# First attention of a fused attention and transformer kernel: score matmuls of 63 and 64 rows instead of 48 and 49

## The chip, the cores and the metric

One core of one Trainium2 chip runs the whole program in one launch. The metric is device time in microseconds (us); lower is better. Engines: PE is TensorE (matmul; PEld are its weight loads), DVE is VectorE, ACT is ScalarE, POOL is GpSimd, SP is SyncE, which only issues DMAs here.

## The reference, cut to what matters

Eight sequences of 512 tokens and 256 channels go through an attention layer with 16 heads of 16 channels, then (not touched here) through two layers of local attention and gated feed-forward.

```python
qkv = x @ w_qkv + b_qkv
q, k, v = jnp.split(qkv, 3, axis=-1)          # 16 heads of 16
a = jnp.einsum('bhsd,bhtd->bhst', q, k)
a = (a + causal_mask) / np.sqrt(HEAD_DIM)
a = jax.nn.softmax(a, axis=-1)
z = jnp.einsum('bhst,bhtd->bhsd', a, v)
z = z.transpose(0, 2, 1, 3).reshape(B, S, D)
...
x = _layernorm(x + z @ w_out + b_out)
```

## The kernel before, in words

**Split operands.** Products that must be close to float32 are made of operands in two parts, high and low. For the scores of the first attention the three products (high by high, high by low, low by high) are stacked along the contraction rows: `Q` holds 16 rows of q high, 16 of q high, 16 of q low, and `Kk` holds k high, k low, k high. These are the slots; `SLOTS = 48` rows hold them. Two heads stand beside each other on the partitions, the even one from row 0, the odd one from row `ODD = 64`. Both tiles have 8 pairs of heads in their second dimension.

**Two passes over the scores.** Step `sm` (L573 to L595 of PE) multiplies one block of 128 queries of a pair by all keys it may see, 48 rows deep (L588, two matmuls, one per head), adds the causal mask by four bfloat16 matmuls of 64 rows (L594), and DVE takes the negative maximum of each row (L468). When the eight blocks of four heads are done, step `mt` turns the maxima on PE (L620), ACT copies them to `mrow` (L421), and SP writes them by four DMAs (L290) into one further row of `Q`, row 48 (and 112), where `Kk` has a row of ones, set by POOL at the start (L322; it sets rows 32 to 63 and 96 to 127 to 1.0, and the slots' loads overwrite 32 to 47). So step `st` (L633, L638), 49 rows deep, gives the transposed scores already shifted by the maximum; ACT takes their exponential into `PT` (L430), POOL zeroes what lies above the diagonal (step `ms`, L345), and step `pv` multiplies by V, 32 matmuls for four heads (L660).

**What sets the order.** The work of all engines is one list of steps written out by hand, `STEPS`; a step `f_...` belongs to the next sequence. Every engine walks the same list with its own part of each step, and semaphores join them. The loop over sequences runs seven times over the list; a first piece (`FIRST`) stands ahead of it and a last one behind. `f_qk` and `f_v` project (L527 to L529), `f_qe` writes q and k parts to `scr` (L265, L267), `f_load` reads them back into `Q` and `Kk` as slots (L283), `z0` to `z3` normalise and turn, `out` projects (L675, L677). `wait_ge(v_set, 3)` holds SP's first load back until DVE's initial memsets are done (V twice, and the padding columns of `Q`, L446).

```python
ODD, SLOTS = 64, 48
...
rows = slice(ODD * hh, ODD * hh + SLOTS)          # sm
...
rows = slice(ODD * hh, ODD * hh + SLOTS + 1)      # st
```

Of the kernel before, what the change touches and what calls it, by code (L numbers as in the profile page):

```python
# [7 lines left out]
F32 = mybir.dt.float32  # L8
# [12 lines left out]
NB, S, DM = 8, 512, 256  # L21
# [36 lines left out]
def wait_apart(eng, K, sem, value):  # L58


    if not isinstance(value, int):
        value = eng.snap(eng.to_reg(value))
        eng.wait_ge(K["made"], MADE)
    eng.wait_ge(sem, value)
# [65 lines left out]
def first_attention(nc, K, scr, w, xin, rows_out, zeros, ahead, x, w_qkv, b_qkv, w_out, b_out, dst):  # L130

    with ExitStack() as ctx:
# [4 lines left out]
        def sem(name):  # L137
            signals.append(nc.alloc_semaphore(name="a_" + name))
            return signals[-1]
# [10 lines left out]

        ODD, SLOTS = 64, 48
        Q, Kk = sb("Q", [P, AH // 2, S + P], F32R), sb("K", [P, AH // 2, S], F32R)

        tri = sb("tri", [P, 2, P], BF16)
# [45 lines left out]
        v_set = sem("v_set")  # L202
# [27 lines left out]
        def steps(eng, do, tail=None):  # L230
            for name, i in FIRST:
                do(name, i, 0)
            with eng.Fori(0, NB - 1) as it:
                for name, i in STEPS:
                    do(name, i, it + 1 if name[0] == "f" else it)
            for name, i in STEPS:
                if name[0] != "f":
                    do(name, i, NB - 1)
                    if tail is not None:
                        tail(name, i)  # L240

        with nc.Block() as block:
            @block.sync
            def _(sp):
                sp.dma_start(xin[:, :, :], x[0].rearrange("(t p) d -> p t d", p=P)).then_inc(x_in, 16)
                for k in range(KT):
                    sp.dma_start(w_raw[:, k, :], w_qkv[P * k:P * k + P]).then_inc(w_loaded[k], 16)
                for n in range(2):
                    sp.dma_start(bqk[:, n::2], b_qkv[DM * n:DM * n + DM].rearrange("(h p) -> p h", p=P),
                                 allow_slow_non_contiguous=True).then_inc(b_loaded, 16)  # L250
                sp.dma_start(bv[:, :], b_qkv[2 * DM:].partition_broadcast(P)).then_inc(b_loaded, 16)
                sp.dma_start(bo[:, :], b_out.partition_broadcast(P)).then_inc(b_loaded, 16)
                wo_rows = w_out.rearrange("(g j d) n -> j d g n", j=HP, d=AD)
                for r in range(2 * HP):
                    sp.dma_start(wo[AD * r:AD * r + AD, :, :], wo_rows[r // 2]).then_inc(wo_loaded, 16)

                def do(name, i, b):
                    if name == "f_x":
                        if not isinstance(b, int):
                            sp.wait_ge(front_full, (b - 1) * NF + 2)  # L260
                            sp.dma_start(xin[:, :, :], x[b].rearrange("(t p) d -> p t d", p=P)).then_inc(x_in, 16)
                    elif name == "f_qe":

                        sp.wait_ge(front_free, b * NE + 1 + i)
                        sp.dma_start(scr[b, 0, P * i:P * i + P], qk_hi[:, i, :].bitcast(F32)).then_inc(parts_out, 16)  # L265
                        sp.wait_ge(lo_done, b * 4 + 1 + i)
                        sp.dma_start(scr[b, 1, P * i:P * i + P], qk_lo[:, i, :].bitcast(F32)).then_inc(parts_out, 16)  # L267
                    elif name == "f_load":

                        wait_apart(sp, K, parts_out, b * 128 + 64 * (i // 2 + 1))  # L270
                        if i == 0 and isinstance(b, int):
                            sp.wait_ge(stacks_set, 2)
                            sp.wait_ge(v_set, 3)
                        if not isinstance(b, int):

                            sp.wait_ge(sc_full, 2 * ((b - 1) * EU + GE * (i + 1)))
                        r0, t0 = 64 * (i % 2), 2 * (i // 2)
                        for t, dst_t, order in ((t0, Q, (0, 0, 1)), (t0 + 1, Kk, (0, 1, 0))):
                            for slot, part in enumerate(order):
                                rows = scr[b, part, P * t + r0:P * t + r0 + 64].rearrange("(h e d) n -> e d h n", e=2, d=AD)  # L280
                                for hh in range(2):
                                    at = ODD * hh + AD * slot
                                    sp.dma_start(dst_t[at:at + AD, PG * i:PG * i + PG, 0:S].bitcast(F32), rows[hh])\  # L283
                                        .then_inc(stacked[i], 16)
                    elif name in ("mt", "f_mt"):
                        sp.wait_ge(mrow_done, b * AG + i + 1)
                        for hh in range(2):
                            at = ODD * hh + SLOTS
                            for p in range(PG):
                                sp.dma_start(Q[at:at + 1, PG * i + p, 0:S].bitcast(F32),  # L290
                                             mrow[2 * p + hh:2 * p + hh + 1, i, :].bitcast(F32)).then_inc(m_in[i], 16)

                def tail(name, i):
                    if (name, i) == FIRST_OF_LAST:
                        sp.wait_ge(parts_out, NB * 128)
                        sp.wait_ge(lo_done, NB * 4)
                        ahead.load(sp, ahead_raw, ahead_wo)
                        zeros.store(sp)
                        sp.wait_ge(front_full, NB * NF)
                        sp.wait_ge(stored, 16)  # L300
                        ahead.first(sp)
                    elif name == "end":
                        zeros.done(sp)

                steps(sp, do, tail)

            @block.gpsimd
# [134 lines left out]
            def _(dve):  # L442
# [6 lines left out]
                def do(name, i, b):  # L449
                    if name == "f_xe":  # L450
# [4 lines left out]
                        if isinstance(b, int):  # L455
                            for kt in range(KT):
                                dve.wait_ge(w_split, kt + 1)
                                dve.tensor_tensor(w_lo[:, kt, :], w_raw[:, kt, :], w_hi[:, kt, :], ALU.subtract)\
                                    .then_inc(w_low, 1)
                    elif name in ("sm", "f_sm"):  # L460
                        p, q = i // TB, i % TB
                        nk = P * (q + 1)
# [48 lines left out]
                def tail(name, i):  # L511
                    if (name, i) in LOW:
                        ahead.low(dve, ahead_raw, ahead_wo, LOW.index((name, i)))
                    elif name == "end":
                        dve.wait_ge(rstd_done, NB)
                        dve.wait_ge(stored, 16 * NB - 16)
                        for t in range(TB):
                            dve.tensor_scalar(out[:, t, :], y[:, t, :], mv[:, t, 0:1], rs[:, t:t + 1],
                                              ALU.subtract, ALU.mult).then_inc(out_done, 1)

                steps(dve, do, tail)

            @block.tensor
            def _(pe):
# [6 lines left out]
                def bank_wait(done, b, units, i, hh):  # L531

                    if not (isinstance(b, int) and b == 0 and i == 0):
                        pe.wait_ge(done, 2 * (b * units + i) + hh - 1)

                def do(name, i, b):
# [37 lines left out]
                    elif name in ("sm", "f_sm"):  # L574
# [9 lines left out]
                            pe.wait_ge(tri_set, 4)  # L584
                            pe.wait_ge(K["made"], MADE)
                        for hh in range(2):
                            rows = slice(ODD * hh, ODD * hh + SLOTS)
                            pe.matmul(bank[:, hh, 0:nk], Q[rows, p, P * q:P * q + P], Kk[rows, p, 0:nk],  # L588
                                      start=True, stop=True)

                        for n in range(2):
                            for hh in range(2):
                                rows, at = slice(ODD * hh, ODD * hh + ODD), P * q + ODD * (hh ^ n)
# [29 lines left out]
                    elif name in ("st", "f_st"):  # L623
# [3 lines left out]
                        if i % GE == 0:  # L627
                            pe.wait_ge(m_in[i // GE], b * 64 + 64)
                        for hh in range(2):
                            rows = slice(ODD * hh, ODD * hh + SLOTS + 1)  # L630
                            bank_wait(exp_done, b, EU, i, hh)
                            if t < 2:
                                m = pe.matmul(SC[hh][:, 0:S - P * t], Kk[rows, p, P * t:P * t + P], Q[rows, p, P * t:S],  # L633
                                              start=True, stop=True)
                            else:
                                for j in (2, 3):
                                    at = 2 * P * (j - 2)
                                    m = pe.matmul(SC[hh][:, at:at + 2 * P], Kk[rows, p, P * j:P * j + P],  # L638
                                                  Q[rows, p, P * j:P * j + 2 * P], start=(j == 2), stop=True,
                                                  skip_group_check=True)  # L640
                            m.then_inc(sc_full, 1)
# [22 lines left out]
                    elif name == "out":  # L664
# [14 lines left out]
                        m.then_inc(y_full, 1)  # L679

                steps(pe, do)


# [1046 lines left out]
```

## Time and profile before

| | |
|---|---|
| runs | 1996.41, 2001.62, 2005.23 us; median 2001.62 |
| the profiled execution | 1997.55 us, span of its trace 1996.0 us |
| mean granted TensorE clock | 0.922 of full speed |
| busy | PE 90%, DVE 56%, ACT 48%, POOL 47% of the span |
| stages | first attention up to about 515 us, then local attention and feed-forward, twice |

The profiled execution is 4.1 us below the median of the runs. In the page, each digit of a line is the busy share of a fortieth of the span (49.9 us); PEclk is the granted clock in tenths. A granted clock of 1.00 is 2.4 GHz and one of 0.50 is 1.2 GHz; a mean between the two is a stretch that had both.

### The profile page before, as it was taken

To read this page: it belongs to the slowest core of one execution; us is meant where nothing else is said; L and a number is where in the kernel's file an instruction comes from. 1 tells how busy PE (TensorE), PEld (TensorE's weight loads), DVE (VectorE), ACT (ScalarE), POOL (GpSimd) and SP (SyncE) were. 2 spreads that over 40 slices of the span, in tenths; PEclk is the share of its full clock that TensorE was granted. 3 is DMA by queue.
4 is the path that set the end of the run, shared out by engine and by line. 5 is a ranking of instruction groups with operands and counts; after the bars stand their busy time and mean duration, and the time that the engine had idled before them with its cause. 6 is when DMAs were issued, how large, how long until landed. Compare 5 with 4: busy or idle time off the path is not lost. (4 is left out here: it accounts for less than half of the span.)

```text
span 1996.0 us, 42845 instructions
## 1 busy us (share of the span) xinstructions
PE 1787.4 (90%) x14072; PEld 1353.2 (68%) x14072; DVE 1109.8 (56%) x2825; ACT 967.3 (48%) x1898; POOL 934.7 (47%) x923
## 2 busy tenths in 40 slices
PE   5899988898669999999979999599999999789887
PEld 3556655565347777777768888477777777577776
DVE  4566655666467766676523333676676666234343
ACT  2655545554336555555534444265555555333332
POOL 3355444554336655555423333455555555333433
PEclk7898888987779999999979999699999999799998
DMA  4333343334010000000121112100000001121221
GB/s 144 106 115 107 106 122 112 117 109 127 22 33 12 32 32 32 32 32 21 50 58 43 63 63 95 44 12 32 32 32 32 32 21 49 50 70 63 65 74 42
DMA packets 103736, 121.28 MB, mean 61 GB/s; under 512 B 23387, under 2 KB 75781, under 8 KB 103685
## 3 DMA queue, kind: packets, MB, share of 16 engines
q1 hardware_dynamic: 96772, 95.45, 15.7%
q0 software_dynamic: 6912, 25.17, 3.5%
q8 instruction: 29, 0.48, 0.1%
q14 instruction: 23, 0.18, 0.0%
HBM read 82.55 MB, written 37.77 MB: 60 GB/s over the span
## 5 line engine op out<-in xcount | busy, mean ns | idle before, releaser
L468 DVE TENSOR_REDUCE a_negm<-a_x 128x2 f32<-128x256 f32 (+3 forms) x256 | 202.4, 814 | 143.7 <-PE a_x L594 141.5
L430 ACT ACTIVATE a_PT<-a_c 128x384 f32<-128x384 f32 (+1 forms) x384 | 183.7, 522 | 139.7 <-PE a_c L633 84.4
L866 POOL TENSOR_TENSOR work<-work 128x512 f32<-128x512 f32 x128 | 164.5, 1287 | 152.2 <-DVE work L1016 151.0
L1541 DVE SCALAR_TENSOR_TENSOR m_hid<-m_a,mw_b,m_gate 128x512 f32<-128x512 f32 x96 | 71.9, 749 | 244.4 <-ACT m_gate L1479 219.8
L1034 DVE CUSTOM_DVE_ANT_0 l_x<-l_x,window 128x256 f32<-128x256 f32 (+1 forms) x512 | 184.1, 421 | 31.7 <-PE l_x L1131 31.7
L1065 PE MATMUL l_f<-w_hi,tails 128*128 128x512 f32 x384 | 168.8, 440 | 14.2 <-DVE work L1016 11.1
L949 ACT ACTIVATE l_PT<-l_c 128x512 f32<-128x512 f32 (+1 forms) x256 | 125.3, 542 | 87.8 <-PE l_c L1171 84.1
L1436 POOL TENSOR_TENSOR m_hid_lo<-m_hid,m_hid_hi 128x512 fp32r<-128x512 f32 x80 | 102.7, 1291 | 131.3 <-ACT m_hid_hi L1490 131.1
L1066 PE MATMUL l_f<-w_hi,tails 128*128 128x512 f32 x384 | 154.8, 403 | 0.0
L1067 PE MATMUL l_f<-w_lo,tails 128*128 128x512 f32 x384 | 154.1, 401 | 0.0
L880 POOL TENSOR_TENSOR l_PS<-l_PT 128x768 f32<-128x768 f32 x64 | 119.6, 1869 | 58.7 <-ACT l_PT L949 58.7
L1479 ACT ACTIVATE m_gate<-m_g,mw_b 128x512 f32<-128x512 f32 x80 | 54.6, 682 | 185.2 <-PE m_g L1588 185.2
L588 PE MATMUL a_x<-a_K,a_Q 48*128 48x256 f32 (+2 forms) x512 | 119.4, 434 | 18.2 <-DMA a_K<-qk_parts 15.4
L873 POOL TENSOR_TENSOR work<-work,l_inv 128x512 f32<-128x512 f32 x128 | 130.9, 1043 | 0.0
L884 POOL TENSOR_TENSOR l_zl<-l_zt,l_zh 128x512 fp32r<-128x512 f32 x64 | 82.8, 1302 | 100.0 <-ACT l_zh L955 100.0
L345 POOL TENSOR_SCALAR_AFFINE_SELECT a_PT<-a_PT 128x512 f32<-128x512 f32 x128 | 81.0, 657 | 97.1 <-ACT a_PT L430 97.0
L660 PE MATMUL a_f<-a_PT,a_V 128*32 128x512 f32 (+3 forms) x1024 | 101.2, 550 | 26.1 <-POOL a_PT L345 14.8
L916 ACT ACTIVATE work<-l_f 128x512 f32<-128x512 f32 x128 | 76.5, 598 | 91.6 <-PE l_f L1067 72.0
L1188 PE MATMUL l_o<-l_PT,l_V 128*64 128x256 f32 (+1 forms) x1024 | 111.8, 361 | 5.7 <-ACT l_PT L949 5.7
L1011 DVE TENSOR_REDUCE l_ss<-work 128x8 f32<-128x512 f32 x128 | 87.0, 680 | 38.8 <-ACT work L916 38.3
L1065 PEld LDWEIGHTS l_f<-w_hi,tails 128*128 128x128 f32 x384 | 74.3, 194 | 44.4 <-issue 21.8
L633 PE MATMUL a_c<-a_Q,a_K 49*128 49x512 f32 (+1 forms) x256 | 94.3, 518 | 7.3 <-DMA a_Q<-a_mrow 3.1
(240 smaller groups left out, 5091.8 us busy)
## 6 DMA issues: line engine op xcount, KB each, us to landing
a_Q<-qk_parts SPq DMA_DIRECT2D x192, 64.0 KB, 2.1
a_K<-qk_parts SPq DMA_DIRECT2D x192, 64.0 KB, 2.1
qk_parts<-a_qk_hi SPq DMA_DIRECT2D x32, 256.0 KB, 2.1
qk_parts<-a_qk_lo SPq DMA_DIRECT2D x32, 256.0 KB, 2.2
after_attn<-rows_out POOLq DMA_DIRECT2D x16, 512.0 KB, 5.2
xin<-after_attn SPq DMA_DIRECT2D x32, 256.0 KB, 3.1
m_xr<-after_attn SPq DMA_DIRECT2D x16, 512.0 KB, 4.1
xin<-in_L_attn_x SPq DMA_DIRECT2D x8, 512.0 KB, 3.5
```

Source lines behind the costliest of these rows:

```text
L430: nc.scalar.activation(PT[:, p // PG % 2, 2 * (p % PG) + hh, QOFF[t]:QOFF[t] + nq], SC[hh][:, 0:nq], ACT.Exp, scale=AD ** -0.5).then_inc(e ...
L468: dve.tensor_reduce(negm[:, q, 2 * p:2 * p + 2], MX[i % 2][:, :, 0:nk], AX.X, ALU.max, negate=True).then_inc(max_done, 1)
L588: pe.matmul(bank[:, hh, 0:nk], Q[rows, p, P * q:P * q + P], Kk[rows, p, 0:nk], start=True, stop=True)
L866: pool.tensor_tensor(t1[:, par, w, :], t1[:, par, w, :], t2[:, par, w, :], ALU.add)\
L873: pool.tensor_tensor(qk[:, i, w, :].rearrange("p (h d) -> p h d", d=FD), t1[:, par, w, :].rearrange("p (h d) -> p h d", d=FD), inv[:, par, ...
L880: pool.tensor_tensor(PS[:, i % 2], PT[:, i % 2, :, 1:TB, 0:P], PT[:, i % 2, :, 0:TB - 1, P:2 * P], ALU.add).then_inc(ps_done, 1)
L949: nc.scalar.activation(PT[:, p % 2, hh, j:j + 2, :].rearrange("p j q -> p (j q)")[:, 0:nq], SC[hh][:, 0:nq], ACT.Exp, scale=8.0).then_inc( ...
L1034: m = dve.tensor_tensor_reduce(out=o, in0=o, in1=mask, scale=-1.0, scalar=-NEG, op0=ALU.add, op1=ALU.min, accum_out=negm[:, q + t, p // 2, ...
L1065: pe.matmul(o, a_hi, r_hi, start=first, stop=False)
L1066: pe.matmul(o, a_lo, r_hi, start=False, stop=False)
L1067: return pe.matmul(o, a_hi, r_lo, start=False, stop=last)
L1188: pe.matmul(OB[rows, P * j:P * j + nq], V[:, j, FD * h:FD * h + FD], PT[:, i % 2, hh, j, 0:nq], start=(j == 0), stop=(j == TB - 1), skip_g ...
```

## The change

`SLOTS` goes; the shift moves to row 63 (and 127), `SHIFT = 63`. Step `sm` reads rows 0 to 62 (64 to 126), step `st` rows 0 to 63 (64 to 127). DVE writes zeros into rows 32 to 63 and 96 to 127 of `Q` once, before the first load, so rows 48 to 62 of `Q` are zero from then on; `Kk` holds ones there already. The values computed are the same. SP's first load waits for the two new memsets. The list of steps is as before.

```diff
-        ODD, SLOTS = 64, 48
+        ODD, SHIFT = 64, 63
...
                             sp.wait_ge(stacks_set, 2)
-                            sp.wait_ge(v_set, 3)
+                            sp.wait_ge(v_set, 5)
...
-                            at = ODD * hh + SLOTS
+                            at = ODD * hh + SHIFT
...
                                     .then_inc(w_low, 1)
+                            for at in (32, ODD + 32):
+                                dve.memset(Q[at:at + 32, :, 0:S].bitcast(F32), 0.0).then_inc(v_set, 1)
...
-                            rows = slice(ODD * hh, ODD * hh + SLOTS)
+                            rows = slice(ODD * hh, ODD * hh + SHIFT)
...
-                            rows = slice(ODD * hh, ODD * hh + SLOTS + 1)
+                            rows = slice(ODD * hh, ODD * hh + ODD)
```

The one place where an engine's sequence changes is the start of DVE. Its rows of the changed program (the numbers after L are lines of the changed file, 2 or so further down):

```order
L446 MEMSET a_Q 128x8x128
L118 MEMSET zero_row 8x64
L453 TENSOR_TENSOR a_xt_lo<-a_f,a_xt_hi 128x512 x2
L458 TENSOR_TENSOR w_lo<-a_PT,w_hi 128x768 x2
L461 MEMSET a_Q 32x8x512 x2
L470 TENSOR_REDUCE a_negm<-a_x 128x2 x4
```

The row with `32x8x512 x2` is new; before, the first reduction followed `w_lo` directly. All other engines issue what they issued, in the same order.

## Rows read from the trace of the kernel before

**Rows 1.** The page, busy time and the 40 slices: PE and the granted clock.

```profile
PE 1787.4 (90%) x14072; PEld 1353.2 (68%) x14072; DVE 1109.8 (56%) x2825; ACT 967.3 (48%) x1898; POOL 934.7 (47%) x923
...
PE   5899988898669999999979999599999999789887
...
PEclk7898888987779999999979999699999999799998
```

**Rows 2.** Two passes: us; PE, PEld, DVE, ACT, POOL busy; PEclk, DMA share, GB/s.

```profile
176.98:237.90 60.92, 54.76 (x493) 35.52 (x489) 38.09 (x65) 33.63 (x71) 30.66 (x36) 0.89 0.37 112
237.90:299.94 62.04, 55.76 (x492) 35.62 (x488) 38.42 (x65) 33.61 (x71) 30.63 (x36) 0.86 0.37 110
```

**Rows 3.** The same view of the longer stretches at the lower clock.

```profile
93.10:99.90 6.80, 6.80 (x44) 3.83 (x47) 4.97 (x7) 4.57 (x9) 2.27 (x4) 0.50 0.35 90
...
212.60:222.80 10.20, 10.20 (x74) 6.02 (x78) 5.41 (x8) 5.54 (x11) 2.44 (x4) 0.50 0.32 86
...
489.20:499.30 10.10, 8.19 (x52) 3.35 (x50) 2.60 (x3) 2.89 (x6) 6.19 (x9) 0.50 0.16 53
```

**Rows 4.** The same view: stretches before and after changes of the clock.

```profile
209.30:212.50 3.20, 2.19 (x18) 1.39 (x18) 2.41 (x4) 2.12 (x5) 2.78 (x5) 1.00 0.44 164
212.60:215.90 3.30, 3.30 (x25) 2.70 (x25) 2.01 (x4) 2.07 (x4) 0.00 (x0) 0.50 0.45 124
216.10:219.40 3.30, 3.30 (x31) 2.15 (x33) 2.05 (x4) 2.38 (x6) 1.22 (x2) 0.50 0.38 103
...
260.50:263.80 3.30, 2.28 (x30) 1.54 (x30) 1.78 (x4) 0.97 (x3) 0.00 (x0) 1.00 0.71 228
263.90:270.60 6.70, 5.04 (x36) 1.88 (x36) 2.22 (x3) 1.60 (x3) 1.27 (x1) 0.50 0.34 83
1793.10:1796.30 3.20, 2.72 (x11) 2.54 (x12) 0.75 (x1) 1.44 (x3) 1.68 (x2) 0.50 0.39 118
1796.50:1799.80 3.30, 3.30 (x16) 2.54 (x15) 0.18 (x1) 0.99 (x2) 1.74 (x1) 1.00 0.08 24
```

**Rows 5.** PE's groups from 212.6 to 215.9 us, shapes apart.

```profile
L588 PE MATMUL a_x<-a_K,a_Q 48*128 48x256 f32 x3 | 1.5, 520 | 0.0
L633 PE MATMUL a_c<-a_Q,a_K 49*128 49x384 f32 x2 | 1.2, 686 | 0.0
```

**Rows 6.** PE's groups from 1793.1 to 1796.3 us, shapes apart.

```profile
L1610 PE MATMUL m_f<-ident,m_hn 128*128 128x128 f32 x8 | 2.0, 427 | 3.2 <-ACT m_hn L1464 3.2
L1586 PE MATMUL m_a<-m_ht_hi,w_hi 128*128 128x512 f32 x1 | 0.8, 776 | 0.0
```

**Rows 7.** PE's groups from 226.3 to 236 us, at the full clock.

```profile
L588 PE MATMUL a_x<-a_K,a_Q 48*128 48x256 f32 x4 | 0.6, 321 | 0.0
```

**Rows 8.** PE's groups from 650 to 800 us, at the full clock (local attention).

```profile
L1131 PE MATMUL l_x<-l_KH,l_QH 64*128 64x256 f32 x84 | 10.5, 327 | 0.0
```

**Rows 9.** Timeline of the pass from 177 us: turning, V products, a mask.

```profile
216.69 1.01 PE L620 MATMUL a_f<-ident,a_negm 128*4 128x128 f32 x4
...
219.32 4.08 PE L660 MATMUL a_f<-a_PT,a_V 128*32 128x512 f32 x32
...
219.97 1.22 POOL L345 TENSOR_SCALAR_AFFINE_SELECT a_PT<-a_PT 128x512 f32<-128x512 f32 x2 [1.68 <-ACT a_PT L430]
...
223.84 2.36 PE L660 MATMUL a_f<-a_PT,a_V 128*32 128x512 f32 x32
...
226.13 0.60 PE L620 MATMUL a_f<-ident,a_negm 128*4 128x128 f32 x4
```

**Rows 10.** DVE at the start of the program.

```profile
8.01 1.83 DVE L458 TENSOR_TENSOR w_lo<-a_PT,w_hi 128x768 fp32r<-128x768 f32 x2
27.86 2.30 DVE L468 TENSOR_REDUCE a_negm<-a_x 128x2 f32<-128x256 f32 x3 [18.03 <-PE a_x L594]
```

**Rows 11.** SP's queue at the start of the program.

```profile
19.86 2.67 SPq L283 DMA_DIRECT2D a_Q<-qk_parts  x6
```

**Rows 12.** POOL's memsets of K, grouped.

```profile
L322 POOL MEMSET a_K<- 32x4096 f32 x2 | 7.0, 3506 | 0.1
```

## The prediction, made before the changed kernel was run

> **What bounds the kernel now.** I read the page first. PE is busy 90% of the span, every other engine at most 56% [rows 1]. PE's digits are 9 nearly everywhere after slice 12. In slices 2 to 10, the first attention, they are 8 and 9 too, but PEclk there is mostly 8: the clock falls inside a stage in which PE is hardly idle [rows 1]. So the next view is the busy time by stretches. One pass of the loop takes 60.9 or 62.0 us at a mean clock of 0.89 or 0.86; ACT and DVE are busy 34 and 38 us of it [rows 2]. PE is therefore what a pass waits for most of the time, and it is slowed by its clock.
>
> Cutting the stage where the clock changes shows one long stretch at 1.2 GHz per pass, always in the same work: the last score steps of a pass, the turning of the maxima and the V products of step `pv` 2. There are eight: the first is 6.8 us, the six of the loop passes behind it are 10.1 or 10.2 us like the second one shown, the last is 10.1 us [rows 3]. In all but the last PE is busy to the full. It isn't idle and then slow; it is slow while it has work.
>
> **Why it is slow there.** Two neighbouring facts are what the forecast rests on. From 212.6 to 215.9 us PE is busy 3.30 of 3.30 us at 1.2 GHz, and the clock stays down for the next stretch [rows 4]. Its matmuls are those of `sm` and `st`, 48 and 49 rows deep, beside the 64-row mask matmuls [rows 5]. From 1793.1 to 1796.3 us, in the last stage, PE is busy less, 2.72 of 3.20 us with only 11 matmuls, and the clock is at 2.4 GHz right behind it [rows 4]; these matmuls are 128 rows deep [rows 6]. Being busy thus doesn't explain the clock; how much of the array works does. I read the trace so: what the granted clock follows grows with the rows in use, the shallow score matmuls count for little, and now their stretches neither hold the clock nor bring it back. Before the fall at 212.6 stands the same picture: PE busy 2.19 of 3.20 us with the same shallow matmuls [rows 4]. The change makes 48 rows 63 and 49 rows 64, in just this work, by a third.
>
> The Trainium skill, "TensorE: Matmul & The Clock Gate", says in "What's actually happening" that the clock is set by how busy the PE has been recently, and in "Why this matters for your kernels" that one should avoid gaps between bursts of matmuls. By that rule, read as busy time, the change does nothing, and the sum would be 0; the trace speaks against it, since the clock stays down through 10.20 us in which PE was busy 10.20. It stands below as a rival.
>
> **The change, part by part.** (a) *Deeper matmuls.* The number and the columns of matmuls stay. Does one of 63 or 64 rows take longer than one of 48? At the full clock the 48-row one of 256 columns takes 321 ns [rows 7], the 64-row one of 256 columns in local attention 327 ns [rows 8]: taken as nothing.
>
> (b) *The clock of the eight stretches.* Worked out on the one from 212.6 us. The V products of step `pv` 2 take 4.08 us at 1.2 GHz; those of `pv` 3 just behind, the same 32 matmuls at 2.4 GHz, take 2.36 [rows 9]: 1.7 us gained. The next V products wait for the mask of 219.97 us (1.22 us long), which moves up with the scores [rows 9], so the 1.7 us isn't lost there. Ahead of them lie 6.7 us of scores and turning (212.6 to 219.3). Turning alone would shrink from 1.01 to 0.60 us [rows 9]. But scores are evacuated by DVE and exponentiated by ACT, which are busy 2.01 + 2.05 and 2.07 + 2.38 us there [rows 4]; so the 6.7 us can't go below about 4.5, the busy time of ACT: a gain of 0 (if ACT's and DVE's chain is the bound already) to 2.2. I take the middle, 1.0 rounded down. That is 2.7 us for each of seven stretches; in the last of the eight PE is only busy 8.19 of 10.1 us [rows 3], so I count the V products' 1.7 alone. Sum 7 x 2.7 + 1.7 = 20.6 us. I don't expect every stretch to stay up: `pv` fills only 32 columns for each head and is itself thin, and the stretch may still start after a wait. I keep four fifths: 16.5 us.
>
> (c) *The second fall.* In two of the passes (62.0 us instead of 60.9, [rows 2]) the clock also falls before step `pv` 1: PE waits for loads and is busy 2.28 of 3.30 us, then runs the V products at 1.2 GHz, 5.04 us busy of 6.7 [rows 4]. The matmuls ahead of that fall are again shallow. Kept up, these two passes give the difference, 62.0 - 60.9 = 1.1 us each: 2.2 us.
>
> (d) *The zeros.* Two memsets of 32 x 4096 on DVE. POOL's of that shape take 3506 ns [rows 12]; DVE has none of it before, so I bound it: 3.5 us each if the engines are alike, half of it if DVE writes faster, twice if the two share a path to memory. They begin when `w_lo` is done at 9.84 us [rows 10] and end at 16.9 us (13.3 to 23.9). What waits for them is SP's first load, issued at 19.86 us [rows 11], and behind it the whole first sequence; DVE's own next work comes at 27.86 us, after an idle time of 18 us [rows 10]. Cover: 3.0 us. Cost 0, at worst 23.9 - 19.9 = 4.0 us.
>
> (e) *The shift row* lands on partition 63 instead of 48, by the same four DMAs of the same size in the same place of SP's queue: nothing.
>
> Sum: 16.5 + 2.2 - 0 = 18.7 us. The profiled execution took 1997.55 us, so it would take 1978.9. The median of the runs is 4.1 us above the profiled one; on that scale the forecast is **1983 us**, 0.9% faster. About 0.5%, 10 us, is what a measurement of this kernel can tell from no change.
>
> **Rivals.**
>
> *Nothing changes* (chance 0.21): the clock follows busy time alone, or the rows are counted in coarse groups in which 48 is already 64. Then (b) and (c) are zero: 2001.6 us. For it: row groups of the array are coarse, and the mask matmuls between are 64 deep already. Against it: rows 4 and 5; two heads' matmuls side by side, each counted as 64 rows, would have the whole array working for 10 us, and the clock still stayed down.
>
> *Only part of it counts* (0.13): only the 64-row step `st` weighs more and the 63-row step `sm` does not, or the clock comes back a stretch earlier but falls all the same. Then some half of (b): 2001.6 - 9 = 1993 us.
>
> *Slower: the falls move* (0.05). PE finishes the score steps sooner and then waits longer for what has its own pace: SP's loads, DMA share 0.71 where PE waits before `pv` 1 [rows 4]. The clock then falls in these waits in every pass, and the dense projections behind them, now at 2.4 GHz, start at 1.2. A stretch of 3.3 us fully busy would take 6.6: 3.3 us in each of seven passes, and 1.1 us for `pv` 1 in the five that don't pay it now, 28.6 us against a gain of 16.5: about 2014 us. It decides from the point where a pass loses more than 2.4 us in new slow stretches. Against it: dense projections bring the clock back quickly in the trace, and the waits follow PE's own progress.
>
> **How the numbers follow.** Forecast 0.61, the rivals 0.21, 0.13 and 0.05. Low end: every stretch stays up with the full 1.7 + 2.2 = 3.9 us, 7 x 3.9 + 1.7 + 2.2 = 31 us, from 2001.6: 1970, and 1 more for the spread of the runs: 1969. High end: nothing changes, with the upper edge left out of a spread of 3.6 us: 2003. The likeliest case has its own range of 1969 to 1991. Faster by over 0.5%: 0.92 of the forecast's 0.61, and a third of the partial case's 0.13: 0.60. Slower by over 0.5%: the slower rival, 0.05. Within 0.5%: the rest, 0.35.
>
> **What would show it.** Right: in the page PEclk of slices 2 to 10 at 9 nearly throughout; the stretch of the last score steps and `pv` 2 at 1.00, its V products near 2.4 us instead of 4.1; passes of some 58 to 59 us; the two memsets of 3.5 us each and the first load still at about 19.9 us; the later stages unchanged. Wrong: eight stretches of 10 us at 0.50 as before (the first rival), short ones in half of the passes (the second), or a lower clock in the projections (the third). If the clock is up and the passes still take 61 us, my reading of PE as the bound is what failed.

## The result, and the profile after

The changed kernel takes 1987.33 us (median of 5 runs, 1986.01 to 1988.42), the kernel before 2001.62 us; the ratio is 0.9936 with a 95% interval of 0.9918 to 0.9953. A second measurement beside the experiments gave 0.9937 (0.9923 to 0.9950), 1987.39 against 1997.57 us. So 10 to 14 us were gained by the one or the other median, 13 us by the ratio. The profiled execution took 1988.02 us, 9.5 less than that of before. One execution of e4 below (2216.92 us, mean granted clock 0.721) and one of e10 (2427.11 us, 0.638) were in a slow state of the chip and are left out of the ratios.

The page after, lines as in [rows 1]:

```profile
PE 1776.7 (89%) x14072; PEld 1345.0 (68%) x14072; DVE 1116.5 (56%) x2827; ACT 968.0 (49%) x1898; POOL 934.4 (47%) x923
...
PE   5889998899679999999979998699999999788887
...
PEclk7898988998789999999979999799999999799998
```

In the first twelve slices PEclk rose by one digit in slices 5, 9, 10 and 12, in and just behind the first attention, and fell in none. The later stages have their old digits but for slice 26, where a stage ends; it reads 7 instead of 6 in e1 below too, which has no deeper matmul. Passes of the loop (us of the stretch and its length; PE, PEld, DVE, ACT, POOL busy; granted clock, DMA share, GB/s), as in [rows 2]:

```profile
57.10:117.60 60.50, 55.62 (x488) 35.26 (x488) 36.59 (x58) 33.23 (x69) 23.52 (x29) 0.87 0.36 106
...
178.00:236.40 58.40, 53.11 (x493) 33.83 (x489) 37.94 (x65) 33.59 (x71) 30.60 (x36) 0.94 0.39 117
...
296.90:357.70 60.80, 54.53 (x490) 35.26 (x488) 38.00 (x65) 33.53 (x71) 30.61 (x36) 0.89 0.37 113
357.70:417.20 59.50, 51.97 (x494) 33.75 (x488) 38.13 (x65) 33.60 (x71) 30.60 (x36) 0.94 0.38 115
```

The first pass in the kernel before, for comparison:

```profile
56.66:116.35 59.69, 54.94 (x489) 34.52 (x489) 36.51 (x58) 33.07 (x69) 25.05 (x30) 0.89 0.36 108
```

The six passes against their lengths before: 60.5 us (59.7 before), 60.4 (60.6), 58.4 (60.9), 60.5 (62.0), 60.8 (60.9), 59.5 (62.0). The first one is thus 0.8 us longer and its clock lower, the second and fifth gained next to nothing, and 6.6 us of gain came in the third, fourth and sixth. The same view of a stretch in the first pass and of the end of the passes, as in [rows 3]:

```profile
80.00:90.30 10.30, 8.46 (x62) 3.77 (x62) 3.83 (x5) 2.83 (x5) 1.27 (x1) 0.50 0.46 142
...
151.70:161.90 10.20, 10.10 (x68) 6.88 (x72) 6.79 (x9) 7.05 (x15) 3.32 (x6) 0.50 0.30 83
213.50:223.70 10.20, 10.15 (x125) 5.87 (x129) 8.56 (x13) 6.36 (x13) 3.79 (x7) 1.00 0.37 95
274.70:281.30 6.60, 6.60 (x50) 3.59 (x52) 4.14 (x6) 3.83 (x8) 2.44 (x4) 0.50 0.27 72
332.70:342.80 10.10, 10.10 (x74) 5.85 (x77) 5.37 (x7) 5.33 (x11) 2.44 (x4) 0.50 0.36 89
394.20:400.80 6.60, 6.60 (x48) 3.97 (x50) 5.22 (x7) 4.70 (x10) 1.78 (x3) 0.50 0.39 108
```

At 213.5 us, in the pass from 178.0, the whole stretch stands at 1.00. At 151.7 and 332.7 us it is as long and as slow as before. At 274.7 and 394.2 us it is 6.6 us instead of 10.1. The stretch at 80.0 us is not of this kind: it is the one in which PE waits for loads and `pv` 1 follows, and in windows of 0.2 us it was 7.0 us long before (79.4 to 86.4). The long stretch of the first pass, at 93.1 us before, is gone.

Where the long stretch is gone in the third and in the last pass, one of 3.4 us at the lower clock has come ahead of it, 28 us into the pass, under the V products of `pv` 1. Here they are in the third pass, before and after:

```profile
204.64 2.36 PE L660 MATMUL a_f<-a_PT,a_V 128*32 128x512 f32 x32 [1.69 <-ACT a_part_f L402]
```

```profile
205.69 3.93 PE L662 MATMUL a_f<-a_PT,a_V 128*32 128x512 f32 x32 [1.70 <-ACT a_part_f L402]
```

PE's groups in the good stretch (compare [rows 5, 7]), and its timeline (compare [rows 9]):

```profile
L635 PE MATMUL a_c<-a_Q,a_K 64*128 64x384 f32 x4 | 1.7, 436 | 0.1
L590 PE MATMUL a_x<-a_K,a_Q 63*128 63x256 f32 x5 | 1.4, 336 | 0.0
```

```profile
217.33 0.60 PE L622 MATMUL a_f<-ident,a_negm 128*4 128x128 f32 x4
...
218.84 2.36 PE L662 MATMUL a_f<-a_PT,a_V 128*32 128x512 f32 x32
...
219.70 1.22 POOL L345 TENSOR_SCALAR_AFFINE_SELECT a_PT<-a_PT 128x512 f32<-128x512 f32 x2 [0.61 <-ACT a_PT L430]
...
221.64 2.36 PE L662 MATMUL a_f<-a_PT,a_V 128*32 128x512 f32 x32
```

The two shapes have their 63 and 64 rows, and 256 columns take 336 ns, where they took 321 with 48 rows in [rows 7]. With more of them the difference goes: in stretches at the full clock `st`'s matmuls of 384 columns take 431 ns with 49 rows (223 to 260 us before) and 430 with 64 (221 to 250 us now), those of 256 columns 328 and 326. Turning takes 0.60 us, where it took 1.01, each set of V products 2.36, and the second begins 2.8 us after the first, where it was 4.5 us. The start of DVE, and of SP's loads (compare [rows 10, 11]):

```profile
7.97 1.83 DVE L458 TENSOR_TENSOR w_lo<-a_PT,w_hi 128x768 fp32r<-128x768 f32 x2
10.71 3.47 DVE L461 MEMSET a_Q<- 32x4096 f32 x1 [0.91 <-issue]
15.09 3.47 DVE L461 MEMSET a_Q<- 32x4096 f32 x1 [0.91 <-issue]
28.14 2.30 DVE L470 TENSOR_REDUCE a_negm<-a_x 128x2 f32<-128x256 f32 x3 [9.57 <-PE a_x L596]
```

```profile
18.04 0.33 SPq L267 DMA_DIRECT2D qk_parts<-a_qk_lo  x1
20.11 2.67 SPq L283 DMA_DIRECT2D a_Q<-qk_parts  x6
```

The memsets take 3.47 us each, with 0.91 us of "issue" ahead of each, and end at 18.56 us. The first load goes out at 20.11 instead of 19.86 us; the store ahead of it (18.04) is itself late by 0.24 us, and the load follows it by 2.07 us, before by 2.06. So it waited for the store and not for the zeros. Where the stage ends is told by the last weight load of `out`, first in the kernel before, then in the changed one:

```profile
L675 PEld LDWEIGHTS a_f<-a_wo_hi,a_zt x128: 186/188/331, 111.0 to 538.9; 128*128 128x128 f32 x128
```

```profile
L677 PEld LDWEIGHTS a_f<-a_wo_hi,a_zt x128: 186/188/330, 111.5 to 529.1; 128*128 128x128 f32 x128
```

538.9 became 529.1 us: the 9.8 us less in the stage are the whole difference of the two profiled executions. Of it 6.0 us came in the six full passes (366.2 us from 56.7 on in the kernel before, 360.1 from 57.1 on now; granted clock 0.87 and 0.90), 4.2 us in the last pass and the piece behind it, and 0.4 us were lost at the start.

### The profile page after: what moved, and what is told of

Read it like the earlier page. It is cut to its first block and busy times, and to the rows that moved or that the text cites. A ratio compares the mean times of both kernels' runs of the same rounds, so it can differ in the third digit from the quotient of the medians.

```text
span 1986.6 us, 42847 instructions
## 1 busy us (share of the span) xinstructions
PE 1776.7 (89%) x14072; PEld 1345.0 (68%) x14072; DVE 1116.5 (56%) x2827; ACT 968.0 (49%) x1898; POOL 934.4 (47%) x923
## 5 line engine op out<-in xcount | busy, mean ns | idle before, releaser
L590 PE MATMUL a_x<-a_K,a_Q 63*128 63x256 f32 (+2 forms) x512 | 114.0, 420 | 16.1 <-DMA a_K<-qk_parts 13.3
L635 PE MATMUL a_c<-a_Q,a_K 64*128 64x512 f32 (+1 forms) x256 | 91.0, 500 | 7.6 <-DMA a_Q<-a_mrow 3.1
```

## The experiments

All ratios are against the kernel before, run on the same chip in turn with it (three chips in all); its median there was 1997.4 to 1998.4 us. The clock is the median over a kernel's executions of the mean granted clock of each; for the kernel before it was 0.923 to 0.924.

| run | what it is | median us | ratio | interval | clock |
|---|---|---|---|---|---|
| e1 | zeros alone, rows 48 and 49 | 1997.43 | 0.9996 | 0.9987 to 1.0005 | 0.924 |
| e2 | `st` 64 rows, `sm` 48 | 1992.78 | 0.9971 | 0.9961 to 0.9981 | 0.928 |
| e3 | `sm` 63 rows, `st` 49 | 1991.40 | 0.9965 | 0.9951 to 0.9979 | 0.928 |
| e4 | 56 and 57 rows | 1991.93 | 0.9968 | 0.9956 to 0.9979 | 0.928 |
| e5 | the changed kernel again | 1987.39 | 0.9937 | 0.9923 to 0.9950 | 0.931 |
| e6 | rows of ones instead of zeros | 1986.20 | 0.9940 | 0.9927 to 0.9954 | 0.933 |
| e7 | masks of 128 rows, on the change | 1995.87 | 0.9988 | 0.9979 to 0.9997 | 0.938 |
| e8 | masks of 128 rows, on before | 2023.85 | 1.0123 | 1.0107 to 1.0138 | 0.918 |
| e9 | `f_sm` 6 to 15 twice, on the change | 1985.97 | 0.9934 | 0.9921 to 0.9947 | 0.938 |
| e10 | the same on before | 1992.35 | 0.9968 | 0.9958 to 0.9978 | 0.930 |
| e11 | `f_sm` 8 to 13 twice, on the change | 1981.78 | 0.9917 | 0.9903 to 0.9930 | 0.938 |
| e12 | `f_sm` 5 to 10 twice, on the change | 1980.49 | 0.9908 | 0.9893 to 0.9924 | 0.939 |

### e1: the zeros without the rows

```diff
-        ODD, SHIFT = 64, 63
+        ODD, SHIFT = 64, 48
...
-                            rows = slice(ODD * hh, ODD * hh + ODD)
+                            rows = slice(ODD * hh, ODD * hh + SHIFT + 1)
```

> Only the two memsets and SP's wait for them; the score matmuls keep 48 and 49 rows, the shift its row 48. Theory (the rows of the score matmuls move the clock): as before, 1996 to 2005 us, with the eight long stretches at the lower clock, 8.0 us at most 10.2 us each. Rival (the change only shifts the work against the clock's own changes, by its 0.3 us later start): near the changed kernel, 1985 to 1990 us, since this start is the same.

1997.43 us, ratio 0.9996. Its page has the granted clock of before, but for one digit less in slice 2 and one more in slices 10 and 26:

```profile
PEclk7798888988779999999979999799999999799998
```

The memsets, SP's wait and the later start cost nothing and gain nothing. The theory's number held, and the rival, that the start 0.3 us later makes the gain, is out.

### e2, e3, e4: one pass alone, and half of the rows

In e2 `sm` reads 48 rows, `ODD * hh` to `ODD * hh + 47`, and everything else is as changed. In e3 the shift is back on row 48, `st` reads 49 rows, `sm` 63:

```diff
-        ODD, SHIFT = 64, 63
+        ODD, SHIFT = 64, 48
...
-                            rows = slice(ODD * hh, ODD * hh + SHIFT)
+                            rows = slice(ODD * hh, ODD * hh + 63)
...
-                            rows = slice(ODD * hh, ODD * hh + ODD)
+                            rows = slice(ODD * hh, ODD * hh + SHIFT + 1)
```

> The transposed scores are 64 rows deep, the first score pass stays at 48. If both passes weigh by their rows, half of the change's 14 us: 1992 to 1996 us. If only the full 64-row pass counts, all of it: 1986 to 1989 us. If only the 63-row pass counts, none: 2000 to 2003 us.

> The first score pass is 63 rows deep, the transposed one stays at 49 with the shift on row 48, so the maximum here is that of scores which contain the previous shift: the shift is not the right one, the instructions and their sizes are. If both weigh by rows: 1992 to 1996 us. If only the 64-row pass counts: 2000 to 2003 us. If only the 63-row pass: 1986 to 1989 us.

0.9971 and 0.9965, so 0.29% and 0.35%, together 0.64%, where the changed kernel has 0.63% (e5). Each figure has an interval of about 0.1% to either side, so that they add up is shown to that width only. Both passes count, the one of 63 rows no less than the one of 64. Their clocks, e2 and then e3:

```profile
PEclk7899888997779999999979999799999999799998
```

```profile
PEclk7888898998789999999979999799999999799998
```

e4 sets `SHIFT = 56` and lets `st` read `SHIFT + 1` rows.

> Rows 56 and 57, the shift on row 56: half of the way from 48 to 63. If the weight grows row by row, part of the gain: 1991 to 1997 us, and a mean clock between 0.922 and 0.933. If rows are counted in groups of 32, the time is that of before (2000 to 2003) or that of the changed kernel (1986 to 1989), nothing between.

0.9968, half of the gain for half of the rows. 48, 49, 56, 57, 63 and 64 all lie between 32 and 64, so a count in groups of 32 would have told no difference between any of these kernels. By the medians, what moves the clock grows with the rows also within such a group; e4's interval (0.9956 to 0.9979) lies clear of e1's and of e5's. Its executions spread widely, from 1989.5 to 1997.5 us, and the profiled one is the slowest of them, with the clock of before (0.922).

### e5, e6: what the rows hold

e6 is the changed kernel with one number:

```diff
-                                dve.memset(Q[at:at + 32, :, 0:S].bitcast(F32), 0.0).then_inc(v_set, 1)
+                                dve.memset(Q[at:at + 32, :, 0:S].bitcast(F32), 1.0).then_inc(v_set, 1)
```

> The changed kernel itself beside the next ones, on the same chip. If the two passes weigh separately and add up (e2 took off 5.7 us and e3 7.0 us against 1998.4), 12.7 us less than before: 1985 to 1988 us.

> As the changed kernel, but rows 48 to 62 of Q hold 1.0 instead of 0.0, against the ones of Kk: each score rises by 15 and so does its maximum, which the softmax takes out again. If the number of rows in use moves the clock: as the changed kernel, 1985 to 1989 us. If what the rows hold counts (zeros being cheap to multiply): off it by more than 3 us, faster if live values raise the clock further, slower if they draw power and cost clock.

0.9937 and 0.9940. Rows of zeros do as much for the clock as rows of ones (0.931 and 0.933). Rows of live values were not tried.

### e7, e8: deeper mask matmuls

```diff
-                        for n in range(2):
-                            for hh in range(2):
-                                rows, at = slice(ODD * hh, ODD * hh + ODD), P * q + ODD * (hh ^ n)
-                                m = pe.matmul(bank[:, hh, at:at + ODD], tri[rows, n, :],
-                                              K["identb"][rows, ODD * hh:ODD * hh + ODD], start=False, stop=True,
-                                              skip_group_check=True)
+                        for hh in range(2):
+                            m = pe.matmul(bank[:, hh, P * q:P * q + P], tri[:, 0, :],
+                                          K["identb"][:, :], start=False, stop=True,
+                                          skip_group_check=True)
```

> As the changed kernel, but the causal mask of step sm comes from two matmuls of 128 rows and 128 columns instead of four of 64 and 64: the same sums. The array takes 128 columns more in each of 256 steps, 53 ns at 2.4 GHz, 13.6 us if PE were the bound in all of them. Theory (rows in use move the clock): the long stretches at 1.2 GHz go in most passes, mean clock of the stage over 0.95, and the time is 1982 to 1992 us, since the clock gives back what the columns take. Rival (busy time alone, or the gain of 14 us was all there is): no better clock, 1994 to 2001 us.

> The kernel before (48 and 49 rows) with the 128-row masks alone. Theory: the clock rises as well though no score matmul is deeper, 1990 to 1998 us. Rival (the effect belongs to the score matmuls' own depth, such as a slower mode of 48-row matmuls): 2000 to 2012 us, with the stretches at the lower clock unchanged.

Both missed in time. e7 lies where its rival put it, but not for its rival's reason: its clock did rise, to 0.938 where the changed kernel has 0.931, and to 0.94 in its loop (57.1 to 420 us). The theory had the clock nearly right there, and not that it would give back what the masks take. e8 lies beyond even its rival: 26 us slower than before by the medians, instead of faster. Passes of e8:

```profile
58.00:123.30 65.30, 62.39 (x427) 34.84 (x426) 38.62 (x62) 34.00 (x71) 25.64 (x30) 0.82 0.33 98
123.30:188.60 65.30, 60.87 (x426) 34.71 (x425) 38.68 (x65) 33.76 (x71) 30.77 (x36) 0.84 0.35 105
188.60:253.60 65.00, 60.86 (x425) 34.61 (x426) 38.63 (x66) 33.76 (x71) 30.75 (x36) 0.84 0.34 105
```

PE is busy 61 of 65 us and the clock is lower than before, 0.82 to 0.84. The timeline of e7 shows one step at 2.4 GHz with its successor, and below it the same steps in the changed kernel:

```profile
226.96 0.28 PE L590 MATMUL a_x<-a_K,a_Q 63*128 63x256 f32 x2
227.17 0.29 PE L594 MATMUL a_x<-identb,a_tri 128*128 128x128 bf16 x2
227.39 0.38 PE L590 MATMUL a_x<-a_K,a_Q 63*128 63x256 f32 x2
```

```profile
224.79 0.28 PE L590 MATMUL a_x<-a_K,a_Q 63*128 63x256 f32 x2
224.92 0.23 PE L596 MATMUL a_x<-identb,a_tri 64*128 64x64 bf16 x4
224.99 0.36 PE L590 MATMUL a_x<-a_K,a_Q 63*128 63x256 f32 x2
```

From the score matmuls of one step to those of the next it takes 0.43 us with 128-row masks and 0.20 us with 64-row ones. The 128 further columns are 53 ns of that at 2.4 GHz. The other 0.18 us come at the two places where PE goes from 64-row matmuls to 128-row ones and back: 0.21 us from scores to mask and 0.22 us from mask to scores, against 0.13 and 0.07. If all 256 steps paid these 0.18 us, it would be 46 us of PE, an estimate from this one step. "TensorEngine Tiling (Array Packing)" of the Trainium skill says in "Key Properties" that changing the tiling mode drains the engine; these rows agree, at some 0.09 us each. So neither run tests cleanly what deeper masks do. In e8 the clock fell though the mask matmuls have twice the rows, which the theory by itself doesn't explain. That the changes of mode are the reason is argued, not shown.

The two runs compared with each other do say something: they differ in the rows of the score matmuls, 48 and 49 or 63 and 64 (and the shift's row and the zeros, which cost nothing in e1). With the deeper ones the kernel takes 1995.87 us instead of 2023.85, 28 us less, at a clock of 0.938 instead of 0.918. That is e5's result again, about twice as large.

### e9 to e12: work of no use, without a change of layout

The next question is whether added work alone moves the clock: issue the step's own score matmuls twice, the second pair over the first (`start=True` begins the sums anew), for some steps of each sequence.

```diff
+                        for again in range(2 if name == "f_sm" and 6 <= i <= 15 else 1):
                             for hh in range(2):
                                 rows = slice(ODD * hh, ODD * hh + SHIFT)
```

e10 is that in the kernel before, at its 48 and 49 rows; e11 has `8 <= i <= 13`, e12 `5 <= i <= 10`.

> As the changed kernel, but the score matmuls of f_sm 6 to 15 are issued twice, the second pair over the first: ten times two matmuls more in each of the eight sequences, work of no use, with 1.5 us of columns in each at 2.4 GHz. Theory (what PE's rows do moves the clock, and the clock is worth 2.5 us a pass where the long stretch goes): the long stretches at 1.2 GHz go in nearly all passes, and the time is 1978 to 1988 us, no slower than the changed kernel in spite of the added work. Rival (the clock isn't what the passes wait for): 1.5 us more for each sequence, 1995 to 2002 us.

> The same doubled matmuls in the kernel before, at 48 and 49 rows. Theory: the clock stays up in more passes as well, 1988 to 1998 us, no slower than before. Rival: 12 us more than before, 2006 to 2014 us.

> As e9, but for f_sm 8 to 13 alone, 0.9 us of columns in each sequence. Theory: between the changed kernel and e9 in its clock, 1980 to 1990 us. Rival: 7 us more than the changed kernel, 1992 to 1996 us.

> As e11, with the doubled score matmuls moved three units up: f_sm 5 to 10, 32 to 37 us after the start of a pass, around the place where the clock fell in the kernel before (35.6 us into its pass) and before most of the stretch. If holding the clock ahead of the fall is what counts, as good as e11 (1981.8 us) or better: 1977 to 1985 us. If the scores inside the stretch must carry it, near the changed kernel: 1985 to 1990 us.

All four medians lie in the theory's ranges. e9 is no faster than the changed kernel (0.9934 and 0.9937): its 160 added matmuls cost nothing. The theory had said that the long stretches would go in nearly all passes, and that missed: in windows of 0.2 us the clock is low for 10.2 us each from 80.6, 200.0, 319.6 and 439.0 us. e11's clock isn't between the changed kernel's and e9's either, but equal to e9's. e10 is the plain case: the kernel before, with nothing but work added, gains 0.32%; its granted clock:

```profile
PEclk7899999898689999999979999799999999799998
```

e11 and e12 add six doubled steps instead of ten, and by the medians gain more than e9; e11's interval overlaps with those of e9 and e5. e12, which puts the steps around the place where the clock used to fall, is the fastest: 1980.49 us, 0.92% below before. Its interval of 0.9893 to 0.9924 only touches e5's 0.9923 to 0.9950, and its five executions (1974.6 to 1981.4 us) all lie below the ten of the changed kernel (1983.1 to 1991.5 us). It ran on another chip than e5, where the kernel before took the same time (1997.36 and 1997.57 us). Its page and three of its passes:

```profile
PE 1767.3 (89%) x14168; PEld 1337.9 (68%) x14168; DVE 1114.9 (56%) x2827; ACT 966.8 (49%) x1898; POOL 934.5 (47%) x923
...
PEclk7899999998689999999979999899999999799998
```

```profile
172.50:230.30 57.80, 51.76 (x501) 33.40 (x502) 37.96 (x66) 33.55 (x71) 30.63 (x36) 0.97 0.39 119
230.30:287.80 57.50, 51.88 (x501) 33.45 (x502) 37.98 (x66) 33.55 (x71) 30.62 (x36) 0.97 0.39 119
287.80:346.50 58.70, 53.67 (x501) 34.30 (x502) 37.93 (x66) 33.61 (x71) 30.61 (x36) 0.94 0.39 117
```

The six passes take 56.9 to 58.7 us at a clock of 0.94 or 0.97, with 12 more matmuls in each. e12 beats both kernels and computes the same. These four runs show that added matmuls can raise the clock and shorten the time. They don't tell rows from busy time, since they add both; that is told by e1 to e4.

## Why the prediction was right, and which term was off

The forecast was 1983 us, 18.7 us gained; 1987.3 was measured, 13 us by the ratio. The direction and the mechanism hold: e1 takes the zeros and the start out of the question, e2 to e4 show the gain growing with the rows while the matmuls' count and columns stay, e6 that rows of zeros and of ones do the same, e10 that the clock can be moved by work alone. The first rival (nothing changes, because busy time or groups of rows are what counts) is out by e2, e3 and e4. The rival "only part of it counts" is out in its first form by e2 and e3, each of which has its half. Its second form, the clock falls all the same, is what happened in some of the passes. The slower rival came in a part of its mechanism, though not in its time: falls moved to `pv` 1, and the first pass is 0.8 us longer. In all, the six full passes gained 6.0 us, where (b) and (c) together had counted 15.2 for them.

- (a) Deeper matmuls cost nothing: right, 430 ns against 431 for 384 columns.
- (b) The value of one stretch, 2.7 us: the pass from 178.0 us is 2.5 us shorter, but not by this sum. The V products of `pv` 2 gave their 1.7 us, 2.36 us for 4.08. The piece ahead of them, from the end of `pv` 1's V products, takes 9.2 us instead of 12.3 (209.6 to 218.8 now, 207.0 to 219.3 before): 3.1 us, where 1.0 was counted. 1.2 us of it are two waits of PE that are gone, 0.80 for the shift's DMA and 0.37 for ACT. Against it `pv` 1's own V products take 1.6 us longer (3.93 for 2.36), and 0.7 us more pass behind the second set. That the sum is near to 2.7 is in part luck.
- (b) "I keep four fifths": this is the step that was mis-sized. Of the eight stretches three are gone (in the first pass, in that from 178.0 and in the one that begins at 417.2), two fell from 10.1 to 6.6 us, and three are still about 10 us long. (The prediction says that all eight lie in the same work. The one at 489.2 us doesn't: it is in the piece behind the loop, under a turning and V products that wait for POOL's mask. And the first one, only 6.8 us long, was counted like those of 10.) I had seen that the stretch depends on how shallow the work is, and took for granted that a third more rows would lift nearly all of them. How I read the traces now, and no run isolates it: the depth was only brought near the point where the clock turns, since the same work at the same rows stays up in one pass and falls in the next. With e12's added matmuls no stretch at the lower clock in the six passes is over 6.8 us, and the passes come to 56.9 to 58.7 us, where I had written 58 to 59 for the change.
- (c) The second fall, 2.2 us: passes of 62.0 us are gone, and those two are 4.1 us shorter together, but the fall itself is only gone in one. The V products of `pv` 1 take 2.36 us instead of 4.49 in the pass from 357.7 us, and still 4.05 in that from 236.4. They were slow in three passes before (the first one, at 3.64 us, was overlooked) and are in four now: 4.50, 3.93, 4.05 and, in the last pass, 4.05 us. So the fall moved from pass to pass and didn't go.
- (d) The zeros: right in their cost of nothing. They end at 18.6 us, not 16.9, as DVE idles 0.91 us ahead of each; of the cover of 3.0 us 1.3 are left.
- (e) The shift row: nothing, by e1 for the wait and start, and by the changed kernel's four DMAs, which take 2.52 us as before (at 41.82 and 41.52 us).

What stays open: which of the passes keep their clock. In one and the same kernel it differs between passes and between runs (1983 to 1992 us in e5), and no run here controls at what point of a pass the clock's changes fall.

The rule of the Trainium skill that I weighed, "TensorE: Matmul & The Clock Gate", "What's actually happening", by which busy time sets the clock, doesn't hold here as read literally: 10.10 us of 10.10 busy from 332.7 us at 0.50, and 10.15 of 10.20 from 213.5 us at 1.00.

## What to carry to other kernels

Where PE is busy and its granted clock is still low, look at how many rows its matmuls use, and not only for gaps. Filling a shallow contraction up with rows of zeros cost a memset off the path and no matmul time here, and repeating a few cheap matmuls over themselves paid as well. Filling up in a way that changes between 64-row and 128-row matmuls did not: in e7 the clock rose, and the kernel was 8 us slower than with 64-row masks. Measure several executions, for the gain is small and differs from one to the next.

## What the runs showed of the hardware that I had not expected

- Matmuls of no use made the kernel faster: 0.32% on the kernel before (e10), and from 1987.4 to 1980.5 us on the changed one (e12). On the changed one ten doubled steps for each sequence gained nothing (e9).
- Going from 64-row matmuls to 128-row ones or back cost some 0.09 us each in a step of e7 at 2.4 GHz.
- Between e8 and e7, both with 128-row masks, the rows of the score matmuls are worth 28 us, twice what they are worth with 64-row masks.
- Ahead of each of the two memsets DVE is idle for 0.91 us that the profile calls "issue". The earlier memsets at the start of the kernel don't show it: `a_Q` begins at 3.67 us, 0.14 us after the one of 0.11 us at 3.42 us.
